# The expert products of a mixture of linear experts, moved from a phase of their own into the attention phase before it

## The reference, cut to what matters

```python
def _ln(x, g, b, eps=1e-05): ...                 # layer norm over the last axis
def _mha(x, w, b, ow, ob): ...                   # 4 heads of 32, softmax over the L axis, of each n alone
def _moe(x, wg, w1, b1, w2, b2):                 # E = 8 experts, FF = 512
    cap = int(CAP_FACTOR * S) // E               # S = 8192 tokens, cap = 1024
    gates = jax.nn.softmax(xf @ wg, axis=-1)
    idx = jnp.argmax(gates, axis=-1)
    mask1 = jax.nn.one_hot(idx, E, dtype=x.dtype)
    loc = jnp.sum((jnp.cumsum(mask1, 0) - 1.0) * mask1, -1)
    keep = loc < cap                             # only the first 1024 tokens of an expert, in token order
    ...
    h = jnp.einsum('ecd,edf->ecf', disp, w1) + b1
    y = jnp.einsum('ecf,efd->ecd', h, w2) + b2
    out = jnp.where(keep, gate_val * y[slot], 0.0)
```

## Time and profile before

| | us |
|---|---|
| median of three runs | 4943.64 |
| the profiled execution's own time | 4948.74 |
| its span, first to last instruction | 4947.0 |
| PE busy | 4053.3 (82%) |
| PE weight loads busy | 2968.2 (60%) |
| DVE busy | 3187.6 (64%) |
| ACT busy | 1598.7 (32%) |
| POOL busy | 1589.3 (32%) |

### The profile page before, as it was taken

One profiled execution on the slowest core, in us unless ns is written; L12 is line 12 of the kernel. 1 busy time (PEld: TensorE's weight loads), 2 busy tenths in 40 slices (PEclk: granted clock), 3 DMA queues, 4 the chain that ended last, 5 costly groups with the idle time before them and its releaser, 6 DMA issues. The chain is left out here.

```text
span 4947.0 us, 163276 instructions
## 1 busy us (share of the span) xinstructions
PE 4053.3 (82%) x66309; PEld 2968.2 (60%) x66309; DVE 3187.6 (64%) x6119; ACT 1598.7 (32%) x2983; POOL 1589.3 (32%) x2521
## 2 busy tenths in 40 slices
PE   6999999666389989899899898998999768885444
PEld 5666666433266767767677777776777656663221
DVE  3777777477466766667676666676765435553777
ACT  1222222144233434434344333343443223331000
POOL 1333333211044444444445444454454310000000
PEclk6999999889689999999999999999998755556677
DMA  0222222256312222222222222222222100002110
GB/s 23 50 57 43 43 55 51 48 142 156 107 36 48 52 44 46 48 53 48 50 43 51 46 48 46 46 56 46 47 51 45 26 18 18 18 18 60 32 32 23
DMA packets 677599, 243.70 MB, mean 49 GB/s; under 512 B 528088, under 2 KB 642464, under 8 KB 676512
## 3 DMA queue, kind: packets, MB, share of 16 engines
q1 hardware_dynamic: 668448, 229.56, 21.3%
q10 hardware_dynamic: 8448, 4.20, 0.3%
HBM read 150.70 MB, written 82.86 MB: 47 GB/s over the span
## 5 line engine op out<-in xcount | busy, mean ns | idle before, releaser
L1373 POOL TENSOR_TENSOR d_f<-d_ms,d_mhalf 128x16 f32<-128x16 f32 x64 | 239.5, 3743 | 959.3 <-DVE d_ms L1807 959.3
L1567 PE MATMUL d_pa<-d_wv,d_hs 128*128 128x512 f32 x1024 | 528.8, 665 | 0.7 <-DVE d_qk L1778 0.4
L1761 DVE SCALAR_TENSOR_TENSOR d_acc<-d_pa,d_cq,d_acc 128x512 f32<-128x512 f32 x576 | 431.7, 749 | 94.7 <-ACT d_acc L1406 79.7
L1383 POOL TENSOR_TENSOR d_prod<-d_ablk,d_tblk 128x15 f32<-128x15 f32 (+7 forms) x960 | 343.2, 357 | 220.1 <-DMA d_ablk<-a_blocks 149.1
L1387 POOL TENSOR_TENSOR d_tblk<-d_tblk,d_prod 128x28 f32<-128x28 f32 (+7 forms) x896 | 344.0, 384 | 70.7 <-POOL d_prod L1383 0.2
L1567 PEld LDWEIGHTS d_pa<-d_wv,d_hs 128*128 128x128 f32 x1024 | 222.9, 218 | 238.9 <-issue 227.2
L1542 PE MATMUL d_pa<-d_hq,d_wqk 128*128 128x259 f32 x768 | 250.8, 455 | 81.9 <-DVE d_acc L1761 59.0
L1580 PEld LDWEIGHTS d_pb<-d_of_head,d_sqT 128*128 128x128 f32 x2048 | 246.2, 196 | 39.1 <-issue 38.9
L1406 ACT ACTIVATE d_acc<-d_pa,d_cq 128x512 f32<-128x512 f32 x192 | 132.0, 688 | 412.7 <-PE d_pa L1542 409.8
L262 POOL TENSOR_TENSOR a_act<-a_act,a_cws 128x512 f32<-128x512 f32 x128 | 166.8, 1317 | 304.9 <-DMA a_cws<-cw_rows 155.9
L1370 POOL TENSOR_TENSOR d_nr<-d_n,d_half_power 128x16 f32<-128x16 f32 x64 | 186.9, 2921 | 204.7 <-DVE d_n L1846 192.6
(11 more groups left out here) (371 smaller groups left out, 9708.6 us busy)
## 6 DMA issues: line engine op xcount, KB each, us to landing
a_cws<-cw_rows SPq DMA_DIRECT2D x32, 1024.0 KB, 10.6
decays<-g_dec SPq DMA_DIRECT2D x16, 2048.0 KB, 7.3
d_dd<-decays SPq DMA_DIRECT2D x64, 512.0 KB, 4.0
d_hs<-h_t SPq DMA_DIRECT2D x512, 32.0 KB, 2.2
t_blocks<-d_tblk SPq DMA_DIRECT2D x128, 128.0 KB, 1.7
a_blocks<-d_at SPq DMA_DIRECT2D x512, 16.0 KB, 1.8
d_ablk<-a_blocks SPq DMA_DIRECT2D x64, 128.0 KB, 2.1
d_tt<-t_blocks SPq DMA_DIRECT2D x512, 16.0 KB, 1.9
```

The source lines that it names most:

```text
L1373: pool.tensor_tensor(f[:, :], ms[:, :], mhalf[:, :], ALU.pow).then_inc(sem("f_ready"), 1)
L1383: link(pool.tensor_tensor(prod[:, 0:n, 0:s + 1], ablk[:, s, s + 1:SB].unsqueeze(2).to_broadcast([P, n, s + 1]), tblk[:, 0, s, 0:s + 1].uns ...
L1567: last = pe.matmul(pa[:, B + m, :], hs[:, u % 2, t, :], wv[:, t, cols(m)], start=(t == 0), stop=(t == TAPS - 1))
L1761: last = dve.scalar_tensor_tensor(out=own, in0=raw(e)[:, :, t:t + QT], scalar=cq[:, t, col:col + 1], in1=own, op0=ALU.mult, op1=ALU.add)
```

## The change

1. The expert products move into the attention phase. Pass i of its loop does the scores, exponentials and values of unit i, the output matrix, norm and choice of unit i-1, q, k and v of unit i+1, and now also the expert products of unit i-2, so two passes more run at the end. The products are not limited by capacity there: each chunk is multiplied with all eight experts, in two halves of one 512-column matmul each, into a single bank `xp`. After each half ACT multiplies the four 128-column blocks by their gates (`weigh`, four instructions), before PE may write the bank again. The bias rows are one more matmul group and a ninth block; DVE sums the nine blocks of a chunk (`reduce`). The sum goes to a new DRAM buffer `moe`.
2. The eight halves are laid between the other steps: PE has them between the turning of the probabilities of different heads, ACT between its exponentials and copies.
3. Merging the expert weights is done once, at the end of pass 0.
4. PSUM is laid out anew: one bank `turned` for all turns, the bias rows and the logits; `qb` for q, v and the wout result; `kb` for k and the attention output; four for scores; `xp`. q, k and v now wait for each other's evacuation. The scores run chunk by chunk with the heads inside. DVE takes the row maxima in two halves instead of one.
5. The last phase, `capacity_phase`, has no products. It loads the route table first (now only the eight marks per token), counts, and makes one number `keep` per token, 1 or 0. Then per sequence it loads moe, y and x, computes moe * keep + y, norm, + x, store. Three buffers are used, and `gather(s + 1)` stands before `finish(s)`.

```diff
+                def weigh(half):
+                    c, e0 = half // 2, NE // 2 * (half % 2)
+                    act.wait_ge(sem("products"), HALVES * (i - 2) + half + 1)
+                    for e in range(e0, e0 + NE // 2):
+                        last = act.activation(part[:, c, e, :], xp[:, (e - e0) * D:(e - e0 + 1) * D], ACT.Identity,
+                                              scale=rt[:, m % 2, 1, c, e:e + 1])
+                    last.then_inc(sem("weighed"), 1)
...
+                def experts(half):
+                    c, e0 = half // 2, NE // 2 * (half % 2)
+                    hold(sem("weighed"), HALVES * (i - 2) + half)
+                    pe.matmul(xp[:, :], yT[:, m % 2, c * P:(c + 1) * P], w12[:, e0:e0 + 4, :].rearrange("p e d -> p (e d)"),
+                              start=True, stop=True).then_inc(sem("products"), 1)
...
+                def reduce(c):
+                    dve.wait_ge(sem("weighed"), HALVES * (i - 2) + 2 * c + 2)
+                    dve.tensor_reduce(moe[:, c, :], part[:, c, :, :].rearrange("p e d -> p d e"), AX_X, ALU.add)\
+                       .then_inc(sem("reduced"), 1)
...
-                for j in range(AH):
-                    rows = slice(AHD * j, AHD * j + AHD)
-                    for c in range(NC):
-                        here = slice(c * P, (c + 1) * P)
-                        last = pe.matmul(ps[4 + j][:, here], qT[rows, here], kT[rows, here], start=True, stop=True)
+                    for c in range(NC):
+                        here = slice(c * P, (c + 1) * P)
+                        for j in range(AH):
+                            rows = slice(AHD * j, AHD * j + AHD)
+                            last = pe.matmul(s4[j][:, here], qT[rows, here], kT[rows, here], start=True, stop=True)
...
+            def gather(s):
+                for c in range(NC):
+                    last = dve.scalar_tensor_tensor(out=mo[:, n, c, :], in0=mo[:, n, c, :], scalar=keep[:, s * NC + c:s * NC + c + 1],
+                                                    in1=yt[:, n, c, :], op0=ALU.mult, op1=ALU.add)
+                ...                      # statistics, variance + eps
+            def finish(s):
+                ...                      # scale, ln2_g, ln2_b, + x
+            gather(0)
+            for s in range(NSEQ):
+                if s + 1 < NSEQ:
+                    gather(s + 1)
+                finish(s)
```

More of the change, by code:

```diff
@@ L1992, in _ @@
[L1992 to L2001, removed]
+            for to, of in ((w1s[:, :, :].rearrange("p k d -> p (k d)"), w1_rows),
+                           (w2s[:, :, :].rearrange("p k d -> p (k d)"), w2_rows),
+                           (b1s[:, :], b1_t), (b2s[:, :], b2)):
+                sp.dma_start(to, of).then_inc(sem("expert_weights"), 16)
@@ L2032, in _ @@
+            steps(pool, iteration)
         @block.scalar
         def _(act):
[L2034 to L2041, removed]
@@ new lines, in iteration @@
+                soften(0)
+                weigh(1)
+                if main:
+                    act.wait_ge(sem("biases"), i - 1)
+                    act.activation(part[:, :, NE, :], tiles(turned), ACT.Copy).then_inc(sem("bias_taken"), 1)
+                soften(1)
+                weigh(2)
+                soften(2)
+                turn(0)
+                weigh(3)
+                soften(3)
+                turn(1)
+                weigh(4)
+                turn(2)
+                weigh(5)
@@ new lines, in iteration @@
+                if main and isinstance(p, int) and i == 2:
+                    hold(sem("b12_ready"), 1)
+                if main:
+                    hold(sem("yT_ready"), i - 1)
+                experts(0)
+                if past:
+                    hold(sem("oT_ready"), i)
+                    if now:
+                        hold(sem("v_used"), i + 1)
+                    for c in range(NC):
+                        last = pe.matmul(qb[:, c * P:(c + 1) * P], oT[:, c * P:(c + 1) * P], wout[:, :],
+                                         start=True, stop=True)
+                    last.then_inc(sem("mixed"), 1)
@@ new lines, in iteration @@
+                experts(7)
+                if then:
+                    hold(sem("hT_ready"), i + 2)
+                    hold(sem("residual"), i)
+                    pe.matmul(qb[:, :], win[:, 0:D], hT[:, :], start=True, stop=True).then_inc(sem("q_ready"), 1)
+                if past:
+                    hold(sem("y_ready"), i)
+                    if main and not then:
+                        hold(sem("bias_taken"), i - 1)
+                    turn(y, sem("y_turned"))
+                if then:
+                    if now:
+                        hold(sem("on_ready"), i + 1)
+                    pe.matmul(kb[:, :], win[:, D:2 * D], hT[:, :], start=True, stop=True).then_inc(sem("k_ready"), 1)
+                    hold(sem("qT_ready"), i + 2)
+                    for c in range(NC):
+                        last = pe.matmul(qb[:, c * P:(c + 1) * P], hT[:, c * P:(c + 1) * P], win[:, 2 * D:3 * D],
+                                         start=True, stop=True)
+                    last.then_inc(sem("v_ready"), 1)
@@ L2163, in _ @@
+                if past:
+                    hold(sem("yT_ready"), i)
+                    for c in range(NC):
+                        last = pe.matmul(turned[:, c * NE:(c + 1) * NE], yT[:, k % 2, c * P:(c + 1) * P], wgs[:, :],
+                                         start=True, stop=True)
+                    last.then_inc(sem("logits"), 1)
+                if isinstance(p, int) and i == 0:
+                    merge_weights()
+            steps(pe, iteration)
         @block.vector
         def _(dve):
-            dve.wait_ge(sem("weights"), 16 * 8)
+            dve.wait_ge(sem("weights"), SMALL)
```

760 lines of the change are left out of this document (394 added, 366 removed).

## The result

The kernel after takes 4649.32 us (median of four runs, 4633.35 to 4655.05) against 4943.02 beside it: ratio 0.9409, 95% interval 0.9371 to 0.9447, some 294 us faster.

What follows compares the result with a forecast made beforehand. PE, mostly at 1.2 GHz, was taken to bound the attention loop and DVE the expert loop. Attention 672 us plus capacity phase 122 make 794 against 977.2, -183, so 4761 us; range 4675 to 4860.

Steps and rivals of the forecast that it cites:

- Which clock: Attention unit: two gapless PE stretches reach full clock, saving 5.5 us; the middle, alternating with ACT waits, gains 1.4.
- the term of 36.5 us per unit: Attention loop: time per unit with expert products inside, 33 to 41; fourteen units make 511 us.
- the 43.4: Attention unit wholly at 1.2 GHz: middle of 45 us with scores at their present rate and 42 with packed scores.
- four microseconds in: Each gapless PE stretch of a unit goes to full clock after 4 us; 4.9 and 6.3 us of work then halve.
- Clock mostly full: Rival, attention loop: 512-column products keep the clock up, DVE bounds at 28 to 32 us per unit, 4642 to 4698; 13%.
- The scores packed: Attention unit: scores chunk by chunk with heads inside fall from 5.2 to about 2.0 us; 1 to 2.8 at full clock.
- The scaled copies: ACT's weighing by gates: between 0.27 and 0.385 us per 128x128 copy, 0.30 taken; 10.0 us per unit.
- the two iterations behind the last unit: End of attention: nothing covers the ping-pong over bank `xp`; sixteen halves of 3.36 us and a sum, 56 us.
- The capacity phase: Last phase: setup 19 us, sixteen sequences of 6.2 making 99, end store 3.5; 122 us in all, 115 to 145.
- Clock low: Rival, attention loop: waits for ACT keep the clock low, 42 to 45 us per unit, 4838 to 4880; 16%.
- Ping-pong not hidden: Rival, attention loop: PE waits for ACT at every product over the one bank `xp`; 57.5 us per unit, 5055; 4%.
- Transfers: Rival, capacity phase: bound by transfers at half the rate, 7.1 us per sequence, 14 us more; no chance of its own.

Runs made afterwards that it cites:

- e6: Kernel after with the four middle expert products of a unit's eight (halves 2 to 5) cut from 512 to 128 columns; 4694.62 us, ratio 0.9506.
- e5: Kernel after with the first two and last two expert products of a unit's eight cut from 512 to 128 columns; 4641.13 us, ratio 0.9395.
- e7: Kernel before with scores packed, the wait for `v_used` moved ahead and twelve useless 512-column products added per attention unit; 4887.66 us, ratio 0.989.
- e4: Kernel after with all eight expert products of a unit cut from 512 to 128 columns; 4680.77 us, ratio 0.9471.
- e8: Kernel after with two banks for products behind the last unit; in the capacity phase, normalisation on ScalarE and bias add on GpSimd; 4612.12 us, ratio 0.9336.
- e10: e9 with four buffers instead of three in the capacity phase; 4591.22 us, ratio 0.9318.
- e9: e8 with the bias add moved from GpSimd back to VectorE; 4607.67 us, ratio 0.9337.
- e2: Kernel before with its scores packed, run chunk by chunk with the four heads inside; 4936.47 us, ratio 0.9986.
- e1: Kernel after with its scores run head by head again, as before; 4659.62 us, ratio 0.944.

## Why the prediction failed

**The step that failed is "Which clock", and by it the term of 36.5 us per unit.** It said that in the middle, where products and turns alternate with waits for ACT, the clock would be low and little gained, and took 5.5 and 1.4 off the 43.4. The clock was 0.99 over the loop and a unit 28.8: over 14 units 108 us of the 119 that the attention and capacity phases lie below their sum of 794. I read the clock of the old middle as a property of waits between groups. The runs say otherwise: with the same waits left standing, the clock falls when the middle products are cut (e6) and mostly stays when the others are (e5).

Half of the step was right. In the middle a full clock gains little: a product comes every 3.01 us (2.9 in the prediction), with the short products of e6 at half clock too, and every 3.37 where whole ones ran at half (4362.08 to 4365.45 in e5). The error was what stands behind the middle. The values, the last products, q and k were priced as largely at half clock, and they run at full. Nor did "four microseconds in" fit the old loop: its values, 6.87 us on end, ran at 0.50.

How much of the 7.7 us is the clock can be estimated from e6, whose 0.70 is inside the 0.65 to 0.8 of the prediction. Its 34.2 and the 0.36 more that each of four steps would take with whole products (3.37 less 3.01) make 35.6. By that about 6.8 are the clock, and under 1 us was too much in the 43.4.

The rival that came true, "Clock mostly full", had 13%. Its number, 28 us, was worked out as a ring over DVE, and 28.4 was measured. That it came so near is partly luck: the wait in front of the choice that closed this sum is not among the new loop's waits, one of 1.9 for the weighing stands in its place, and e7 has a ring of 27.3 with DVE busy 58%. Its argument, ten 512-column products per unit instead of two, should have led to asking where they lie, not how long the gapless stretches are.

**What was right.** To the first scores 26.3 (26.7). Merging in unit 0, 42.0 (45.6). Unit 1, 26.8 (28). The scores packed: 32 records in 1.17 (1 to 2.8). The scaled copies were cheaper than their range: four in 1.09 to 1.14, and the next instruction follows 1.00 after the first, so 0.25 from start to start (0.27 to 0.385; 0.30 taken). The sums over nine rows 2.14 (2.1 to 2.15). In the two iterations behind the last unit most halves took 3.37 (3.36); these iterations and the last store together were 63.5 (60.7; 91.88 less one unit of 28.4). The capacity phase was 113.4 (122): its setup 15.7 (19, of which 9 for the route table, which took 6.6; the bounds of 4 and 12 on it no run shows), a sequence 5.88 (6.2); the transfers stayed under it, at a share of 0.59. These differences are 11 us together.

**The rivals.** Clock low: out, and e4 and e6 show about what it would have been, 33.0 and 34.2 per unit with less to do. The rule of the Trainium skill that stood beside it ("TensorE: Matmul & The Clock Gate", A second HAM failure mode: micro-idles between groups that cycle through PSUM swing the clock) was not met in 12 of the 13 units of this loop, at 1.00 with eight short waits for ACT per unit, four of them for the bank; it was met in e6, with as many waits and a thinner middle. What decides between the two in general no run here shows. Ping-pong not hidden: out, PE waited 2.4 us per unit for the weighing (31.6 / 13), not 26.9. Transfers: out.

**What stays open.** One unit in 13 (in e8 to e10 two) takes 33.1 with a fall of the clock in the values, the others not; no run tells why that one. Which engine would have to get faster to shorten the unit of 28.4 was not tried.

## What to carry to other kernels

A loop that is 85% busy on PE at half clock isn't a loop with no room. Before pricing added matmuls, ask what they do to the clock in the places where PE waits now, what stands behind those places, and price both ends: here work that fills the waits was free and gave 3 us per unit back, and removing it made a unit longer. Here the wide products were worth most in the thin stretch ahead of other PE work. And after a stage was made shorter, look for what it was hiding: the loads in e9, the exponentials in e2 (PE's wait for them grew from 36.5 to 69.7).

## What was not expected of the hardware

- Taking three quarters of the products' columns away makes a unit 4.2 us longer (e4, 33.0 against 28.8); adding twelve products to a loop, with its scores packed, makes its unit 3.3 us shorter (e7, 27.3 against 30.6).
- Of two cuts of equal size, the one in the middle costs 5.4 us per unit (34.2 against 28.8) and the one at the ends 0.4 (29.2).
- A POOL add of 128x512 (1.37 us) makes four DVE operations beside it take 2.15 instead of 1.14; with it gone they are back (e8, e9). The Trainium skill says in "SBUF — State Buffer", Terms, that VectorE and GpSimd share a port pair which one holds for a whole instruction; by that the four would be held up for up to the add's 1.37 (an estimate), and the trace has 1.0.
- Matmuls of 32 rows and 128 columns in 32-bit take 1.17 us for 32 records when neighbours use different row groups and banks, 2.82 when they don't (e1), both at full clock: 37 and 88 ns per record. The 18 ns of the 64-row blocks were not reached.
